# Attention scores from one-pass fp32r parts instead of full fp32 products, with even and odd heads projected apart

## The reference

```
h = group_norm(x, 32 groups) * gn_w + gn_b      # [C, T] an image
q, k, v = wq h + bq, wk h + bk, wv h + bv
p = softmax(q^T k / 4)  for each head           # block 3: / sqrt(128)
x = x + wp (p v) + bp
```

## Time and profile before

| what | value |
|---|---|
| median of 3 runs | 91.23 us (91.22 to 91.29) |
| the profiled execution's own time | 91.06 us |
| its span, first to last instruction | 89.3 us |
| PE busy, share | 82.3 us, 92% |
| VectorE busy, share | 66.2 us, 74% |
| ScalarE busy, share | 46.4 us, 52% |
| granted TensorE clock | 1.00, the 2.4 GHz level, in every slice |

### The profile page before, as it was taken

How to read it: one execution, slowest core, us unless ns; L and a number is a source line. 1 busy time by engine, 2 the same in 40 slices (tenths; PEclk the granted TensorE clock), 3 DMA queues, 4 the chain that set the end, 5 groups by cost and what they waited for, 6 DMA issues and landing times.

```text
span 89.3 us, 2244 instructions
## 1 busy us (share of the span) xinstructions
PE 82.3 (92%) x820; PEld 60.5 (68%) x820; DVE 66.2 (74%) x173; ACT 46.4 (52%) x110; POOL 7.5 (8%) x21
## 2 busy tenths in 40 slices
PE   5959979999999999999999999999999998988890
PEld 5947858975675787895577456779957456477770
DVE  1467799899527999969993689995996179676841
ACT  2804046882399013669357731348765972446730
POOL 7640000000020001100000200020000000120000
PEclk9999999999999999999999999999999999999999
DMA  1992000000000000000000000000000000000013
GB/s 25 234 341 84 0 0 7 0 0 4 7 0 0 0 0 0 7 4 0 0 7 0 0 0 7 0 0 0 0 7 0 0 0 0 4 7 0 0 29 88
DMA packets 2026, 1.93 MB, mean 22 GB/s; under 512 B 352, under 2 KB 1504, under 8 KB 2016
## 3 DMA queue, kind: packets, MB, share of 16 engines
q1 hardware_dynamic: 1728, 1.71, 6.3%
q10 hardware_dynamic: 288, 0.08, 0.4%
HBM read 1.53 MB, written 0.26 MB: 20 GB/s over the span
## 4 chain that ended last, share of the span: by engine, by line
PE 82%; DVE 7%; issue 3%; ACT 3%; POOL 1%; DVEq 0%; ACTq 0%; POOLq 0%
PE ps L340 17%; PE ps L347 14%; PE ps L459 12%; PE ps L396 8%; PE ps L449 6%; PE ps L429 4%; PE ps L465 4%; PE ps L357 4%; PE ps L410 3%; PE ps L470 2%; PE ps L386 2%; DVE xs L654 2%; ACT probs L545 2%; PE ps L363 2%; PE ps L484 2%
## 5 line engine op out<-in xcount | busy, mean ns | idle before, releaser
L636 DVE TENSOR_REDUCE neg_max<-ps 128x2 f32<-128x512 f32 x48 | 30.4, 682 | 2.9 <-PE ps L340 2.6
L545 ACT ACTIVATE probs<-ps 128x512 f32<-128x512 f32 x48 | 26.1, 600 | 8.9 <-PE ps L449 8.6
L347 PE MATMUL ps<-q,k_even 32*128 32x256 f32 x96 | 16.5, 392 | 0.0
L340 PE MATMUL ps<-k_odd,q 32*128 32x256 f32 x96 | 16.3, 389 | 0.0
L340 PE MATMUL ps<-k_even,q 32*128 32x256 f32 x96 | 16.3, 394 | 0.0
L347 PE MATMUL ps<-q,k_odd 32*128 32x256 f32 x96 | 14.9, 396 | 0.0
L449 PE MATMUL ps<-max_rows,first_rows 32*128 32x512 f32 x48 | 14.8, 521 | 0.0
L459 PE MATMUL ps<-probs,v_heads 128*32 128x256 f32 x192 | 12.7, 385 | 0.2 <-ACT probs L545 0.2
L340 PEld LDWEIGHTS ps<-k_odd,q 32*128 32x128 f32 x96 | 11.4, 184 | 0.7 <-issue 0.5
L347 PEld LDWEIGHTS ps<-q,k_even 32*128 32x128 f32 x96 | 10.8, 184 | 1.1 <-issue 0.7
L340 PEld LDWEIGHTS ps<-k_even,q 32*128 32x128 f32 x96 | 10.5, 184 | 1.4 <-DVE q L616 1.2
(11 more groups left out here) (73 smaller groups left out, 105.3 us busy)
## 6 DMA issues: line engine op xcount, KB each, us to landing
w<-in_w SPq DMA_DIRECT2D x4, 256.0 KB, 4.9
xs<-in_x SPq DMA_DIRECT2D x2, 129.0 KB, 2.5
out<-xs SPq DMA_DIRECT2D x4, 64.0 KB, 1.5
const<-in_constants ACTq DMA_DIRECT2D x1, 65.5 KB, 2.7
ident<-in_identity SPq DMA_DIRECT2D x1, 64.0 KB, 3.4
wv<-in_wv_last SPq DMA_DIRECT2D x1, 64.0 KB, 4.9
vec<-in_vectors ACTq DMA_DIRECT2D x1, 14.0 KB, 2.7
```

Of the source, the lines that this page charges most:

```text
L340: return mm(ps(*step)[:, qc * T:(qc + 1) * T], q[b][of, qc * CHUNK:(qc + 1) * CHUNK], (k_odd if i >= PER else k_even)[b][of, :], start=Tru ...
L347: return mm(ps(*step)[:, kc * T:(kc + 1) * T], (k_odd if i >= PER else k_even)[b][of, kc * CHUNK:(kc + 1) * CHUNK], q[b][of, :], start=kc ...
L545: nc.scalar.activation(probs[b][:, i, :, :].rearrange("p c t -> p (c t)"), ps("scores_t", l, b, i)[:, :], ACT.Exp, scale=SCALE).then_inc(e ...
L636: nc.vector.tensor_reduce(neg_max[b][:, i // PER, :, ROWS * (i % PER)], src, AX_X, ALU.max, negate=True).then_inc(max_done, 1)
```

## The change

Scores of blocks 0 to 2 are no longer fp32 products. They are made from fp32r operands, as `add_max` was before, in two accumulating matmuls for each half of a head:

- q and k are projected twice, once for the even and once for the odd heads (i = 0, 1 of `project_q` and `project_k`). The host writes each head's 16 weight rows twice in a row, so that a group of 32 output rows holds the same head twice.
- `keep_q` (ACT) writes q times a 0/1 column rounded to fp32r: zeros on the first 16 rows, q's high part on the second 16. `store_q` (DVE) subtracts it from q and writes fp32r: the first 16 rows hold q's high part, the second 16 q's low part.
- `store_k_high` (ACT) writes k rounded to fp32r, `store_k_low` (DVE) the rest of k. Both have the same head twice.
- `scores`, `scores_2`, `scores_3`, `scores_end` are four matmuls for a head: half 0 with k_high, half 0 with k_low, half 1 with k_high, half 1 with k_low. `scores_t` to `scores_t_end` likewise.
- A block has six matrices in its weight array instead of four. Block 0's four for q and k come in one DMA and its other two in a second one. `fold_bias` has five instead of three columns in blocks 1 and 2. `scale_w` covers 640 instead of 384 columns there.
- PLAN is another one, with its own order and banks.

Block 3's work is the same, with its own storage (`q_one`, `k_one`).

The core of the diff:

```diff
+                k = (k_high, k_low)[part][b]
+                return mm(ps(*step)[:, qc * T:(qc + 1) * T], q[b][of, i // PER, qc * CHUNK:(qc + 1) * CHUNK],
+                          k[of, i // PER, :], start=part == 0, stop=part == 1)
...
+                k = (k_high, k_low)[part][b]
+                return mm(ps(*step)[:, kc * T:(kc + 1) * T], k[of, i // PER, kc * CHUNK:(kc + 1) * CHUNK],
+                          q[b][of, i // PER, :], start=kc == part == 0, stop=False, skip_group_check=True)
+
+            def qk_stored(l, b, p):
+
+                pe.wait_ge(q_stored, nth("store_q", l, b, p))
+                pe.wait_ge(k_low_stored, nth("store_k_low", l, b, p))
...
+                    nc.scalar.activation(q_kept[b][:, i, :], ps("project_q", l, b, i)[:, 0:T], ACT.Identity,
+                                         bias=folded_low(l, i), scale=low_rows).then_inc(q_kept_ready, 1)
...
+                    nc.scalar.activation(k_high[b][:, i, :], ps("project_k", l, b, i)[:, 0:T], ACT.Identity,
+                                         bias=folded(l, 2 * i + 1)).then_inc(k_high_stored, 1)
...
-                    ts(q[b][:, :], ps("project_q", l, b)[:, 0:T], folded(l, FQ), None, ALU.add).then_inc(q_stored, 1)
+                    dve.wait_ge(q_kept_ready, nth("keep_q", l, b, i))
+                    stt(out=q[b][:, i, :], in0=ps("project_q", l, b, i)[:, 0:T], scalar=folded(l, 2 * i),
+                        in1=q_kept[b][:, i, :].bitcast(F32), op0=ALU.add, op1=ALU.subtract).then_inc(q_stored, 1)
...
+                    dve.wait_ge(k_high_stored, nth("store_k_high", l, b, i))
+                    stt(out=k_low[b][:, i, :], in0=ps("project_k", l, b, i)[:, 0:T], scalar=folded(l, 2 * i + 1),
+                        in1=k_high[b][:, i, :].bitcast(F32), op0=ALU.add, op1=ALU.subtract).then_inc(k_low_stored, 1)
...
-            sp.dma_start(w[0][:, :], weights[0]).then_inc(w_in[0], 16)
+            sp.dma_start(w[0][:, 0:NQK, :], weights[0][:, 0:NQK, :]).then_inc(w_in[0], 16)
+            sp.dma_start(w[0][:, NQK:, :], weights[0][:, NQK:, :]).then_inc(w_rest_in, 16)
```

More of the change, by code:

```diff
@@ L90 @@
-divide 1 0 0; attend 1 0 1 6; row_max 1 1 7; row_max 1 1 1; turn_max 1 1 1 2; turn_out 1 0 1; scores 1 1 2 4
-scores_t 1 1 7 0; scores_t 1 1 5 3; store_max 1 1 1; scores 1 1 0 1; divide 1 0 1; scores_end 1 1 2
-scores_t_end 1 1 7; scores_t_end 1 1 5; scores_end 1 1 0; turn_back 1 0 0; add_max 1 1 6; add_max 1 1 4
-add_max 1 1 7; add_max 1 1 5; row_max 1 1 2; exps 1 1 6; project_out 1 0 0 2; row_max 1 1 0; exps 1 1 4
-fold_bias 2 0 0 6; exps 1 1 7; residual 1 0 0; turn_max 1 1 0 7; add_bias 2 0 0; sum_squares 2 0 0
@@ new lines @@
+project_k 2 1 1 4; row_max 2 0 5; project_q 2 1 0 7; keep_q 2 1 1; store_k_high 2 1 1; project_k 2 1 0 2
+store_q 2 1 1; keep_q 2 1 0; turn_max 2 0 1 0; store_k_low 2 1 1; project_v 2 1 0 1; store_k_high 2 1 0
+store_q 2 1 0; store_max 2 0 1; scores_t 2 0 7 4; add_max 2 0 2; add_max 2 0 0; scores 2 1 5 5
+store_k_low 2 1 0; store_v 2 1 0; scores_t_2 2 0 7; scores_2 2 1 5; scores_t_3 2 0 7; scores_3 2 1 5
+scores_t 2 0 6 7; scores_t_end 2 0 7; scores_end 2 1 5; scores_t 2 0 4 0; scores_t_2 2 0 6; scores_t_2 2 0 4
@@ L137 @@
+residual_one 3 1 0; write 3 1 0
 """
@@ L144, in emptied_by @@
     if kind == "project_k":
-        return [("store_k_even", l, b, i)] + [("store_k_odd", l, b, i)] * (not last)
+        return [("store_k_one" if last else "store_k_low", l, b, i)]
     if kind == "project_q":
```

390 lines of the change are left out of this document (217 added, 173 removed).

## The result

The kernel after the change takes 96.04 us (median of four executions: 94.77, 98.42, 97.32, 94.11) where the one before takes 91.26 us (91.22 to 91.36). The ratio is 1.0347 with a 95% interval of 1.0283 to 1.0411. 90.8 us was forecast, with a range of 88.5 to 93.0. Sign and range were both missed.

The account below looks back on a forecast made before the run. VectorE was taken to bound the stretches, a chain over all engines the seams. Stretches +1.6 and seams -2.0 took the span from 89.3 to 88.9 us; forecast 90.8 us, 0.5% faster, range 88.5 to 93.0.

Parts of the forecast that it names:

- the stretches: First to last row maximum of each of blocks 0 to 2; from 39.21 to 40.8 us, plus 1.6.
- the seams: Rest of the span: start, block 0 to 1, block 1 to 2, end; -0.1, -0.8, -0.4, -0.7, together -2.0 us.
- The gaps kept: VectorE's idle time inside the stretches: a quarter of 3.19 us, 0.8, would stay; range 0 to 3.2.
- rival 1: The gaps stay: image 1's store chain holds its first row maximum; priced at 2.2 us kept, 92.2 us; chance 0.27.
- The bursts of heads "half as long": Score bursts in the seams halve: -0.43 us per four-head burst, -0.6 for image 1's scores_t.
- Rival 4: A pass is not cheaper: fp32's rate, load not hidden or issue too slow; 96.2 us, half lost 93.5; chance 0.08.
- The start: Seam before block 0's first row maximum (10.25 us): one more projection and keep_q against a shorter burst; -0.1 us.
- The end: Seam after block 2's last row maximum (21.70 us): two score bursts of 0.66 us halved, -0.7; exponentials given nothing.
- The projections: 12 more of two full-array passes on TensorE: 5.2 us of array time; +0.43, +0.86, +0.43 in the seams.
- VectorE as the pace of the stretches: VectorE, 92% busy in the stretches, sets their pace; added stores lengthen them, busy time 36.0 to 40.0 us.
- The price of a pass: An fp32r score pass of 256 columns costs 0.11 us, its weight load hidden; saves 10 us of array time.
- The stores: store_q and store_k_low 0.41 us each on VectorE, plus 4.7 us; keep_q 0.57, store_k_high 0.47 on ScalarE, plus 9.

Follow-up runs that it names:

- old_four_pass: Kernel before, its order, each half's scores as four fp32r passes (same operand four times) instead of two fp32 passes: 94.36 us, ratio 1.0343, clock 1.00.
- new_filler: Kernel after with two blank fp32 matmuls added to every turn_max, ahead of its wait for row maxima: 98.97 us, ratio 1.0685.
- new_fewer_waits: Kernel after, TensorE issuing no wait for a semaphore value it has already waited for: 92.31 us, ratio 1.0107.
- old_projections: Kernel before with each project_q and project_k of blocks 0 to 2 issued twice (12 more), nothing else: 95.99 us, ratio 1.0514.
- old_two_pass: Kernel before, scores as two fp32r passes a half instead of two fp32 passes, no low parts or side work: 91.02 us, ratio 0.986.
- old_two_pass_fewer_waits: Kernel before, scores as two fp32r passes a half, no low parts, without TensorE's repeated waits: 90.24 us, ratio 0.9725.
- new_fp32r_projections: Kernel after with q and k projected in fp32r, one pass where they took two: 96.16 us, ratio 1.0431.
- old_one_pass_scores_t_fewer_waits: Kernel before without TensorE's repeated waits, turned scores as one fp32r pass a half, maxima's scores still fp32 products: 89.89 us (88.83 to 98.56).

## Why the prediction was wrong

In the prediction's own terms: it had a span of 88.9 us, and the profiled execution took 93.0. Of these 4.1 us the gaps in the stretches are 3.0 (3.82 for 0.8), VectorE's busy time there 0.2, the seams 0.9 (-1.1 for -2.0). 1.4 of the gaps are the low clock's, and the median execution lost more to it than this one. What is left at the full clock, 2.7 us in the profile or 93.2 - 90.8 = 2.4 by the line, is enough for a kernel that is slower than before and just outside the range. So two things failed: a term that was missing, and two that were mis-sized.

By the experiments, at the full clock: 91.3 before; -2.6 for the short passes (88.7); +8.5 for the side work in the old order (97.2); -4.0 for the order (93.2). The first two are differences of runs, the first of them by a line; the last is what is left over. The lower clock adds 2.9 in the median execution: 96.0.

- **The clock: the step that failed, by absence.** The granted clock was 1.00 in every slice of before, and the prediction took it as given for after. No term and no rival held a fall. The runs show that it falls when the scores' array time is cut: in the old order it is 0.998 or more with the array time of fp32 scores (`old_four_pass` and every kernel with all scores in fp32), 0.92 to 0.98 with two short passes, 0.87 to 0.89 with one. It cost 2.9 of the 4.8 us by which the median rose. The Trainium skill ("TensorE: Matmul & The Clock Gate", section "A second HAM failure mode: psum-queue depth-cycling") tells of a kernel whose clock swings because TensorE often idles briefly between groups of matmuls. The trace agrees in that the longest idle time shown before the fall is 0.57 us. That such idling is the trigger no run here shows, and 0.85 us of it in the same execution passed without a fall.
- **The gaps kept, named the weakest step, failed too.** 0.8 us was forecast and 3.82 measured. 1.4 of them lie in the slow spell; the rest, 2.4, is at rival 1's price of 2.2. That is luck, for rival 1's mechanism does not show at the full clock. It had the store chain of image 1 holding back its first row maximum. The only waits of VectorE for ScalarE's stores inside the stretches are the three of the slow spell, in block 1. In `new_filler` with the clock at 1.00 these stores have none (0.35 us before the row maximum behind them, where before had 0.79), and in block 2 image 1's stores have none either. The gaps outside the slow spell are spread: 0.74 us in block 0, 0.48 in block 1, 1.20 in block 2, most of them waits of 0.2 to 0.4 us for scores. 1.1 us of them go when the repeated waits go: `new_fewer_waits` has 2.68 - 1.39 = 1.3 us outside its slow spell. The range held 93.0 as its upper end, though rival 1's own was 93.2.
- **The bursts of heads "half as long": a term mis-sized.** -0.43 to -0.6 was booked for each. The first burst takes 1.03 us up to the next step, and 0.67 in `new_fewer_waits`: 0.36 us of what was booked is not there. The passes themselves were sized well, and the waits issued between them were left out. Rival 4 named the issue limit, from a burst's 0.06 us a matmul, but as one of matmuls and not of waits. Over the kernel the waits cost 2.2 us, where the kernel before hid all but 1.0 of theirs. They are also why the middle seams gave too little. The seams measured +0.37, -0.06, +0.30 and -1.70 against -0.1, -0.8, -0.4 and -0.7 forecast; without the repeated waits they are +0.36, -0.57, -0.34 and -1.75. The start stays half a microsecond worse than forecast, unexplained. The end is 1.0 better, and so the sum hides how far the first three were off: two of its eight exponentials now come before it (3.14 us of them in the window for 4.16), and the prediction gave that nothing.
- **The projections.** 12 more are 5.2 us of array time. The prediction booked 1.7 of it, in the seams (+0.43, +0.86, +0.43), and nothing inside the stretches. `old_projections` shows nine tenths of it in the old order's time; what it costs in the new order was not run by itself.
- **VectorE as the pace of the stretches: half right.** Its busy time was forecast to 0.2 us, and the sign of the term was right. But leaving out 3.0 us of it gained only 0.8, because VectorE then waited for ScalarE's stores.
- **The price of a pass: right.** The forecast was one column a cycle, 0.11 us. Timeline of the kernel after, turned scores of one head, all in one row group:

```profile
33.39 0.28 PE L400 MATMUL ps<-q,k_high 32*128 32x256 f32 x1
...
33.51 0.28 PE L400 MATMUL ps<-q,k_low 32*128 32x256 f32 x1
...
33.63 0.28 PE L400 MATMUL ps<-q,k_high 32*128 32x256 f32 x1
...
33.75 0.27 PE L400 MATMUL ps<-q,k_low 32*128 32x256 f32 x1
```

They start 0.12 us apart, each behind a weight load of its own, so the load hides although it goes to the same row group. By the rule of the Trainium skill that the prediction weighed ("TensorE: Matmul & The Clock Gate", section "Part 3: Packing small matmuls") they would be 0.21 apart, load plus columns, by the prediction's estimate; the measurement decides against it here.
- **The stores: right.** `store_q` and `store_k_low` take 0.48 us each, and the next instruction starts 0.40 after them where nothing holds it (42.12 to 42.52). In the groups of the kernel after, VectorE's row maxima are unchanged and `store_k_high` costs the 0.48 us of the old plain stores:

```profile
L705 DVE TENSOR_REDUCE neg_max<-ps 128x2 f32<-128x512 f32 x48 | 30.5, 683 | 2.1 <-PE ps L392 1.5
L587 ACT ACTIVATE k_high<-ps,bias 128x256 fp32r<-128x256 f32 x8 | 3.9, 482 | 4.9 <-PE ps L454 4.9
```

**A version that beats both kernels.** `old_fewer_waits`, the kernel before without TensorE's repeated waits, takes 90.27 us: 1.2% faster than before and 6% faster than the median of after, with a clock of 0.998 or more in every execution. The kernels in the old order with two short passes, or with some scores short, reach 88.2 to 89.7 us in their best executions, but their medians lie between 89.9 and 91.6 and single executions took up to 98.6. They also leave out the low parts of q and k, so they do less than either kernel here.

**What stays open.** What exactly makes the clock fall at one place in one execution and not in the next. Why the slopes of the lines used here differ (0.54 to 0.88 us for each us of loss), so that full-clock times near a loss of 1.7 us are good to some tenths, and those of `old_two_pass`, `old_two_pass_fewer_waits` and `new_fp32r_projections` to a microsecond or more. How much of the order's -4.0 us is its own, since its side work was never run in the new order with fp32 scores. And what the 24 ScalarE stores cost in the new order.

## What to carry to other kernels

Before you book a saving on TensorE, ask what the array does with the time: where TensorE would wait for another engine anyway, the gain can come back as a lower clock, and here the fp32 scores without repeated waits (90.27 us) were as fast as the short ones (90.24). Look at the granted clock of every execution, not of one profile. Waits for a value that the engine has already waited for are instructions in the stream and show up between short matmuls; leaving them out changes nothing in the order and gave 1 to 2 us here. And side work on an idle engine is only free if nothing stands directly behind it: 18 stores on a ScalarE that is idle half the time cost 5.5 us.

## What was unexpected of the hardware

- With the same program and input, executions of the kernel after took 94.11 to 98.42 us and of `old_one_pass_scores_t_fewer_waits` 88.83 to 98.56 us, in step with a mean clock of 0.929 to 0.982 and 0.894 to 1.00. Of the kernels with fp32 scores, the widest was the kernel before, 90.95 to 91.58 us over all its executions.
- One fp32r pass a half (93.32 us) was slower than two (90.24 us), both without repeated waits.
- A head's wait instructions before its matmuls delay the next head's first pass to 0.12 us after the last, though every repeated wait has been met. Without the repeated ones the four heads' first passes share one row of 0.39 us in the timeline.
